# Two pieces of VectorE's work trade places in the main loop of a conditioned attention layer

## The reference

```python
h = layernorm(x)
mod = silu(time) @ mod_w + mod_b
shift, scale, gate = split(mod, 3)
h = h * (scale + 1.0) + shift
q, k, v = heads(h @ w_qkv)                      # 16 heads of 32
q = rope(layernorm(q) * q_norm_w); k = rope(layernorm(k) * k_norm_w)
attn = softmax(q @ k.T / sqrt(32))
return x + (attn @ v -> rows) @ w_out * gate
```

## Time and profile before

| | us |
|---|---|
| median of 3 runs | 1784.97 |
| lowest and highest | 1782.56 and 1785.4 |
| the profiled execution, its own time | 1784.8 |
| its span, from first to last instruction | 1783.0 |

### The profile page before, as it was taken

One profiled execution on the slowest core, in us unless ns is written; L12 is line 12 of the kernel. 1 busy time (PEld: TensorE's weight loads), 2 busy tenths in 40 slices (PEclk: granted clock), 3 DMA queues, 4 the chain that ended last, 5 costly groups with the idle time before them and its releaser, 6 DMA issues.

```text
span 1783.0 us, 34594 instructions
## 1 busy us (share of the span) xinstructions
PE 1678.6 (94%) x13342; PEld 1010.2 (57%) x13342; DVE 1274.4 (71%) x1667; ACT 1035.1 (58%) x1610; POOL 635.1 (36%) x708
## 2 busy tenths in 40 slices
PE   5978899999999999999999999999999999999987
PEld 3645456555565555655556555565555655555444
DVE  8766677777777777777777777777777777775553
ACT  3445566566556566656655656665665665655552
POOL 0613234334334424433433442442343343243222
PEclk9979999999999999999999999999999999999999
DMA  6034445545455464554645545455554555543554
GB/s 209 25 66 95 101 107 116 128 107 125 113 117 133 101 138 105 119 125 104 139 102 133 117 104 135 106 128 116 119 121 111 124 114 118 123 110 84 124 122 127
DMA packets 55576, 205.53 MB, mean 115 GB/s; under 512 B 6888, under 2 KB 6888, under 8 KB 39160
## 3 DMA queue, kind: packets, MB, share of 16 engines
q0 software_dynamic: 18288, 133.18, 38.4%
q1 hardware_dynamic: 37128, 70.14, 11.7%
HBM read 53.25 MB, written 16.88 MB: 39 GB/s over the span
## 4 chain that ended last, share of the span: by engine, by line
PE 70%; DVE 23%; issue 4%; DMA 1%; POOL 0%; ACT 0%; SPq 0%; DVEq 0%; POOLq 0%; ACTq 0%
PE Y L357 10%; PE O L458 10%; PE SA L439 9%; PE Y L344 8%; DVE xin L1017 7%; DVE cst L1050 7%; PE Y L347 7%; PE Y L351 6%; PE Y L474 6%; PE SM L396 6%; DVE qk_lo L1039 4%; PE SA L443 2%; DVE stats L984 2%; PE SA L334 1%; DVE cst L1058 1%
## 5 line engine op out<-in xcount | busy, mean ns | idle before, releaser
L1050 DVE TENSOR_REDUCE cst<-SM 128x2 fp32r<-128x1024 f32 x236 | 289.3, 1226 | 295.5 <-PE MB L396 295.3
L807 ACT ACTIVATE probs<-SM 128x1024 f32<-128x1024 f32 x256 | 262.4, 1025 | 237.2 <-PE SM L443 230.7
L1298 POOL DMA_DIRECT2D probs<-probs x127 | 111.0, 874 | 690.1 <-ACT probs L809 624.4
L1050 DVE TENSOR_REDUCE cst<-MB 128x2 fp32r<-128x1024 f32 x236 | 287.2, 1217 | 0.0
L458 PE MATMUL O<-probs,vals 128*32 128x512 f32 x2048 | 272.4, 604 | 0.0
L809 ACT ACTIVATE probs<-SA 128x1024 f32<-128x1024 f32 x256 | 262.4, 1025 | 0.0
L1279 POOL TENSOR_TENSOR pair_part<-rows,rope_pair 128x256 f32<-128x256 f32 x128 | 94.5, 739 | 383.9 <-DVE rows L1027 383.0
L344 PE MATMUL Y<-wqkv_hi,hT_hi 128*128 128x512 f32 x716 | 214.9, 422 | 0.0
L347 PE MATMUL Y<-wqkv_hi,hT_lo 128*128 128x512 f32 x716 | 193.8, 392 | 0.4 <-DVE hT_lo L1033 0.4
L351 PE MATMUL Y<-wqkv_lo,hT_hi 128*128 128x512 f32 x716 | 192.2, 390 | 0.0
L703 ACT ACTIVATE rows<-Y 128x512 f32<-128x512 f32 x121 | 72.6, 600 | 205.7 <-PE Y L351 205.7
(11 more groups left out here) (208 smaller groups left out, 3589.9 us busy)
## 6 DMA issues: line engine op xcount, KB each, us to landing
probs<-probs POOLq DMA_DIRECT2D x127, 1024.0 KB, 7.7
xin<-in_x_dram SPq DMA_DIRECT2D x62, 256.0 KB, 7.4
xres<-in_x_dram SPq DMA_DIRECT2D x60, 256.0 KB, 2.6
out_dram<-xres SPq DMA_DIRECT2D x60, 256.0 KB, 5.5
shift_scale<-mod_rows SPq DMA_DIRECT2D x15, 512.0 KB, 3.8
gate<-mod_rows SPq DMA_DIRECT2D x16, 256.0 KB, 5.5
rows<-in_L_cond_mod_w_dram SPq DMA_DIRECT2D x2, 1024.0 KB, 8.9
probs<-in_L_cond_w_qkv_dram SPq DMA_DIRECT2D x2, 1024.0 KB, 13.2
```

The source lines that it names most:

```text
L807: act.activation(probs[:, a, 2:4, :], SM[:], ACT.Exp).then_inc(s_exp, 1)
L1050: dve.tensor_reduce(heads[:, 2 * half:2 * half + 2, 0], bank[:], AX.X, ALU.max, negate=True).then_inc(max_out, 1)
```

## The change

Both edits are in VectorE's list of the main loop. `low_qk` of the next group, both parts, is now called ahead of `square_sums(s + 5, 0)` and not behind it. `normalize_x(s + 7)` is now called ahead of the fourth maxima, `maxima(s + 1, 3)`, and not behind them. No instruction is added, removed or altered, and the lists of the other engines are the same.

```diff
             for s in range(LAST + 1):
-                if s > 0 and tile(s + 5):
-                    square_sums(s + 5, 0)
                 if group(s + 1):
                     low_qk(s + 1, 0)
                     low_qk(s + 1, 1)
+                if s > 0 and tile(s + 5):
+                    square_sums(s + 5, 0)
...
+                if tile(s + 7):
+                    normalize_x(s + 7)
                 if late(s + 1):
                     late_maxima(s + 1, 3, 0)
                     late_maxima(s + 1, 3, 1)
                 elif group(s + 1):
                     maxima(s + 1, 3)
-                if tile(s + 7):
-                    normalize_x(s + 7)
```

## The result

| | median us | lowest and highest | runs |
|---|---|---|---|
| before | 1785.18 | 1782.56 to 1787.26 | 4 |
| changed | 1746.74 | 1744.31 to 1747.01 | 4 |

The ratio is 0.9782, 95% interval 0.9765 to 0.9799: 38.4 us or 2.2% faster. The forecast was 1759 us, 1.4% faster; the time is that of rival 1, 1747.5 us, and lies 0.7 us above the lower end of the range. The profiled execution of the changed kernel has a span of 1745.2 us (before 1783.0).

A forecast was written before the change was run, and what follows sets the result against it. TensorE was taken as the bound, waiting at L396 for VectorE's low parts. From 1784.8 us, minus 37.3 (Term 1), plus 11.4 (Term 3), the rest zero, came 1758.9, say 1759 us; range 1746 to 1771.

The forecast's parts named there:

- rival 1: VectorE gets in early between GpSimd's instructions before the fourth maxima, so the moved normalisation costs nothing: 1747.5 us, chance 0.28.
- What bounds the kernel: Main loop: TensorE, which waits at L396 for VectorE's low parts (L1039), 0.69 us a step; without it 25.56 us.
- Term 1: At L396: low parts come earlier, so TensorE's wait for them goes; gain 37.3 us.
- Term 2: The sum of squares L984, now behind the low parts, is hidden before the maxima of L396; cost zero.
- Term 3: Normalisation before the fourth maxima: GpSimd delays it, maxima start 0.35 us later, L417 loses 0.20 a step; cost 11.4 us.
- What else moves: GpSimd's L1284 and L1287 held up about 0.3 us each, its DMA later, SP's loads keep their room; cost zero.
- Rivals 2 and 3: 2: VectorE shut out until the second L1287 ends, 1829 us, chance 0.08; 3: next wait takes half, 1772 us, 0.10.
- rival 2: Before the fourth maxima VectorE waits until the second L1287 ends; L417 loses 1.43 us a step: 1829 us, chance 0.08.

The follow-up runs named there:

- norm_moved_alone: The changed kernel with the first sum of squares put back ahead of the low parts, so only the normalisation is moved; 1748.21 us, ratio 0.9791.
- wait_then_dma_issue: The kernel before, with a wait for half of the fourth maxima and a small GpSimd DMA issue added ahead of L1292; 1815.10 us, ratio 1.0157.
- filler_035: The changed kernel with fillers (two of 512 columns, one of 128) between normalisation and fourth maxima, to start these 0.35 us later; 1749.33 us, ratio 0.979.
- three_fillers: The changed kernel with three unused statistics instructions of 512 columns between normalisation and fourth maxima; 1768.92 us, ratio 0.9915.

## Why the prediction was right, and where it wasn't

**What bounds the kernel, right.** The step of the opening without the wait, 25.56 us, told what TensorE alone needs; the changed kernel's steps are 25.58.

**Term 1, right in mechanism and size.** 37.3 us were forecast for the wait; the stretch of 53 steps lost 36.65 us, and L396 is at 0.97 behind L458. The low parts are ready 0.6 us before, as worked out. The first exponentials did not take over.

**Term 2, right.** L984 is hidden with 0.56 us (0.6 forecast), and costs nothing. But `norm_moved_alone` shows that its move, and that of the low parts with it, brings nothing beside the other half: I never asked what each half is worth alone, though the earlier trace rows had it (fourth maxima to 807.10, high parts from 809.34, a hole of over 2 us for an instruction of 0.68).

**Term 3, wrong: 11.4 us forecast, none measured.** The forecast gain was 26 us and 38.4 came; nearly all of the difference is this term. It failed at two places, and with either of them right it would have come to nothing.

- The boundaries. I sorted them by the gap in the records, and carried over from L1292 and L1311 that one without a gap is closed. The carried case was a special one, since L1298, a DMA issue, stood directly ahead of it; the earlier trace rows leave that row out. L1017 entered behind L1287, L1020 behind L1306, and the end of L1020 was 0.97 us ahead of the fourth maxima. Rival 1 had this course and its time, but for a reason (the small overlap) that `wait_then_dma_issue` refutes, where a boundary with an overlap of 0.05 us was closed. The Trainium skill says (SBUF — State Buffer, "Who interferes with whom") that whoever issues first has the shared port for the whole instruction. The changed kernel agrees at both boundaries (VectorE ended 0.56 and 0.54 us behind the GpSimd instruction), and in an opening step, where L1306 was issued at 197.62 and L1017 at 197.63, L1017 sat out L1306 and took 1.82 us. Directly behind a DMA issue the starts in the records don't follow that rule: L1017 was issued at 807.01 and L1311 at 807.27, and L1311 went first.
- The conversion. The maxima ending 0.35 us late were to cost 0.20, by the start of the weight load L417 at 807.30. The row of the matmul was the one to read, 0.42 us behind the end of the maxima (807.10); `filler_035` puts the cost at nothing.

```profile
807.52 0.46 PE L417 MATMUL SA<-ident_r,cst 128*128 128x128 f32 x4
```

**What else moves, right.** GpSimd's DMA issue comes later in the step, 1.58 us before L417 and not 2.12, and TensorE waits for that DMA 1.6 us in all (before 1.8); the loads of SP didn't show up either. It was L1306 and L1279 that were held up, not L1284 and L1287.

**Rivals 2 and 3 did not come.** The turning point of rival 2, a start of the maxima 0.84 us late, was too near: `three_fillers` has 0.75 and is still 0.85% faster than before. An estimate from the 0.37 us of room and the 0.69 of the wait puts it at 1.06 us; no run tried it.

**The chances.** 0.52 went to a forecast with a loss in it that did not come, and 0.28 to the right time. The range held, by 0.7 us, since it took in rival 1; the mechanism that the forecast gave to the moved normalisation was wrong.

## What to carry to other kernels

Before an instruction is moved, ask why it is long where it stands: L1017 had 2.37 us, of which 1.6 were a wait for a port, and shortening that wait by 0.73 us (one semaphore wait on the other engine) brought about as much as moving it. Here the wait was 0.69 us: each edit that moved the late instruction up by that much took it all, and a second one beside it brought nothing; price each half alone. And when a case is carried from one place in the trace to another, look one instruction further back than the pair that is compared.

## What the runs showed of the hardware that was not expected

- VectorE (two inputs in SBUF) and GpSimd (reading SBUF) meet at a port, and not only at semaphores as the first section has it. They take turns there instruction by instruction, also where GpSimd's next instruction is issued before the last has ended (overlap 0.03 to 0.05 us): VectorE ended 0.54 to 0.56 us behind the GpSimd instruction, in every middle step of the changed kernel. Directly behind a GpSimd DMA issue it sat out two instructions: 2.37 us before, 2.93 with a DMA issue put there, 2.52 at another pair of instructions; with a memset of 0.51 us in between it didn't (1.41). In one instance it was let in there all the same (1.71), where VectorE's own pass ran until 0.38 us past the issue of the GpSimd instruction.
- The lead of a weight load over its matmul, 0.22 us for L417 while TensorE is busy, doesn't add to a wait: in `three_fillers` both started 0.05 us behind the releasing instruction.
